# A scan layer's product of state and C, issued on GpSimd as two halves by state with a signal each

## The reference, cut to what matters

```python
dA = jnp.exp(delta[..., None] * A)                        # 512 channels x 16 states
dB = delta[..., None] * Bp[:, :, None, :] * x[..., None]
def step(h, inp):
    dA_t, dB_t, C_t = inp
    h = dA_t * h + dB_t
    return (h, jnp.einsum('bdn,bn->bd', h, C_t))          # y = sum over the 16 states of h * C
...
y = ys + x * D_skip
y = y * jax.nn.silu(z)
return x + jnp.einsum('bli,di->bld', y, out_proj_w)
```

## Time and profile before

| | us |
|---|---|
| median of 3 runs | 461.95 |
| lowest and highest | 460.28 and 463.77 |
| the profiled execution's own time | 461.22 |
| its span, first to last instruction | 459.4 |
| around the span | 1.8 |
| TensorE busy | 399.4 (87%) |
| VectorE busy | 355.5 (77%) |
| GpSimd busy | 291.6 (63%) |
| ScalarE busy | 265.3 (58%) |

### The profile page before, as it was taken

One profiled execution on the slowest core, in us unless ns is written; L12 is line 12 of the kernel. 1 busy time (PEld: TensorE's weight loads), 2 busy tenths in 40 slices (PEclk: granted clock), 3 DMA queues, 4 the chain that ended last, 5 costly groups with the idle time before them and its releaser, 6 DMA issues.

```text
span 459.4 us, 8117 instructions
## 1 busy us (share of the span) xinstructions
PE 399.4 (87%) x2607; PEld 250.9 (55%) x2612; DVE 355.5 (77%) x735; ACT 265.3 (58%) x561; POOL 291.6 (63%) x325
## 2 busy tenths in 40 slices
PE   4999999999999996887699899997779977988874
PEld 2676766767575753443354445464447644556543
DVE  1577877777896789238599997697887799998895
ACT  1466556786957763489652566748441834326563
POOL 0255546364546442229995597989998899994820
PEclk9999999999999999899799999999999999999989
DMA  6960101010100000019400000166000000000001
GB/s 226 389 239 25 47 0 49 1 46 1 49 2 1 1 2 0 1 30 250 114 2 0 0 2 25 55 164 149 0 0 1 2 0 2 0 0 2 11 24 57
DMA packets 22764, 22.64 MB, mean 49 GB/s; under 512 B 1058, under 2 KB 20258, under 8 KB 22212
## 3 DMA queue, kind: packets, MB, share of 16 engines
q1 hardware_dynamic: 22164, 21.65, 15.0%
q10 hardware_dynamic: 560, 0.49, 0.3%
HBM read 21.02 MB, written 1.12 MB: 48 GB/s over the span
## 4 chain that ended last, share of the span: by engine, by line
PE 48%; issue 16%; POOL 15%; DVE 14%; DMA 3%; ACT 1%; SPq 0%; DVEq 0%; POOLq 0%; PEldq 0%; ACTq 0%
POOL both L1649 8%; PE ps L636 7%; PE ps L645 7%; PE ps L444 6%; PE ps L405 5%; PE ps L416 4%; DVE both L1375 3%; PE ps L471 3%; PE ps L505 3%; PE ps L432 3%; POOL both L1602 2%; DMA both<-bounce 2%; DVE zst L1441 2%; PE ps L663 2%; DVE xc L1342 2%
## 5 line engine op out<-in xcount | busy, mean ns | idle before, releaser
L1649 POOL TENSOR_TENSOR both<-both 128x1024 f32<-128x1024 f32 x64 | 149.8, 2361 | 20.1 <-DVE both L1375 19.8
L1375 DVE TENSOR_TENSOR_SCAN both<-both,ps 128x1024 f32<-128x1024 f32 x64 | 144.2, 2277 | 23.4 <-PE ps L636 13.5
L1014 ACT ACTIVATE both<-delta,a_neg 128x504 f32<-128x504 f32 x120 | 74.2, 703 | 39.1 <-DVE both L1375 39.1
L1602 POOL TENSOR_SCALAR both<-both,rden 128x256 f32<-128x256 f32 x128 | 60.1, 484 | 50.7 <-DVE rden L1230 50.7
L645 PEld LDWEIGHTS ps<-con,both 128*128 128x128 f32 x512 | 55.6, 142 | 62.8 <-POOL both L1649 39.8
L645 PE MATMUL ps<-con,both 128*128 128x128 f32 x512 | 70.8, 282 | 13.8 <-POOL both L1649 13.8
L636 PE MATMUL ps<-both 64*128 64x512 f32 x256 | 73.3, 649 | 7.3 <-DVE both L1375 5.8
L887 ACT ACTIVATE both<-both,negmax 128x256 f32<-128x256 f32 x128 | 63.2, 498 | 20.8 <-DVE negmax L1223 20.8
L1223 DVE CUSTOM_DVE_ANT_0 both<-ps,both 128x256 f32<-128x256 f32 x128 | 46.6, 419 | 11.3 <-PE ps L405 11.0
L444 PE MATMUL ps<-both 128*128 128x512 f32 x64 | 33.4, 646 | 6.3 <-DMA both<-in_ctx_t 6.3
L416 PE MATMUL ps<-con,both 128*128 128x128 f32 x256 | 38.5, 277 | 0.0
(11 more groups left out here) (136 smaller groups left out, 611.2 us busy)
## 6 DMA issues: line engine op xcount, KB each, us to landing
both<-bounce SPq DMA_DIRECT2D x16, 512.0 KB, 5.7
both<-in_ctx_t SPq DMA_DIRECT2D x8, 512.0 KB, 3.3
both<-in_wg SPq DMA_DIRECT2D x1, 1024.0 KB, 8.8
both<-in_wu SPq DMA_DIRECT2D x1, 1024.0 KB, 11.0
both<-in_wd SPq DMA_DIRECT2D x1, 1024.0 KB, 12.9
win_sb<-in_win SPq DMA_DIRECT2D x1, 1024.0 KB, 14.8
resid<-in_x SPq DMA_DIRECT2D x1, 896.0 KB, 6.6
both<-in_wkv SPq DMA_DIRECT2D x1, 512.0 KB, 3.8
```

The costliest lines, as they stand in the source:

```text
L1014: act.activation(da[sl % 2].rearrange("p (a s n t) -> p a s n t", a=GT, n=HN, s=2)[:, :, :, n, 1:L], delta[:, idx % RING_X].rearrange("p ( ...
L1375: dve.tensor_tensor_scan(h_sb[:, hu % RING_H], da[e.slot % 2][:, e.tt * HU:(e.tt + 1) * HU], bank(2 * (hu % 2), 2), 0.0, ALU.mult, ALU.add ...
L1602: pool.tensor_scalar(s, s, rden[:, u, q:q + 1], 1.0, ALU.mult, ALU.mult).then_inc(normed, 1)
L1649: pool.tensor_tensor(g_sb[:, hu % RING_G].rearrange("p (n s t) -> p s n t", n=HN, s=2), h_sb[:, hu % RING_H].rearrange("p (s n t) -> p s n ...
```

## The change

`weigh` issues two products instead of one: the first for states 0 to 3 of the round's 8, the second for states 4 to 7. Each is 128 x 512 elements, and each adds one to the semaphore `g_ready`, which now counts two to a round. `accumulate` waits for the first half before its first transpose and for the second half before its fifth. VectorE's scan, which waits for the buffer of three rounds before, and the reload of `cb` for the second group wait for both halves. Nothing else moves.

```diff
@@ SyncE, reload of cb @@
-                            sp.wait_ge(g_ready, count((NC - 1) * NH * GT + b + 1))
+                            sp.wait_ge(g_ready, count(2 * ((NC - 1) * NH * GT + b + 1)))
@@ accumulate @@
-                pe.wait_ge(g_ready, count(hu + 1))
                 for n in range(HN):
+                    if n % (HN // 2) == 0:
+                        pe.wait_ge(g_ready, count(2 * hu + 1 + n // (HN // 2)))
                     mm = pe.matmul(bank(4 + e.idx % 2)[:, e.tt * P:(e.tt + 1) * P], g_sb[:, hu % RING_G, n * P:(n + 1) * P], ident, start=False,
                                    stop=e.nh == NH - 1 and n == HN - 1, is_transpose=True, skip_group_check=True)
                 mm.then_inc(y_acc, 1)
@@ scan @@
-                dve.wait_ge(g_ready, count(hu - RING_H + 1))
+                dve.wait_ge(g_ready, count(2 * (hu - RING_H + 1)))
@@ weigh @@
-                pool.tensor_tensor(g_sb[:, hu % RING_G].rearrange("p (n s t) -> p s n t", n=HN, s=2),
-                                   h_sb[:, hu % RING_H].rearrange("p (s n t) -> p s n t", n=HN, s=2),
-                                   cb[:, e.nh, e.tt].rearrange("p (n s t) -> p s n t", n=HN, s=2), ALU.mult
-                                   ).then_inc(g_ready, 1)
+                for part in range(2):
+                    ns = slice(HN // 2 * part, HN // 2 * (part + 1))
+                    pool.tensor_tensor(g_sb[:, hu % RING_G].rearrange("p (n s t) -> p s n t", n=HN, s=2)[:, :, ns],
+                                       h_sb[:, hu % RING_H].rearrange("p (s n t) -> p s n t", n=HN, s=2)[:, :, ns],
+                                       cb[:, e.nh, e.tt].rearrange("p (n s t) -> p s n t", n=HN, s=2)[:, :, ns],
+                                       ALU.mult).then_inc(g_ready, 1)
```

## The result

| us | before | after |
|---|---|---|
| median of 4 runs each | 461.86 | 466.02 |
| lowest and highest | 460.28 and 463.77 | 464.30 and 466.54 |
| ratio, with its 95% interval | | 1.0092 (1.0059 to 1.0125) |
| the profiled execution, its span | 461.22, 459.4 | 464.30, 462.5 |

One of its twelve executions took 774.59 us, at a granted clock of 1.00; it is left out of the ratio, and nothing here explains it. The forecast was 465.2, so both measurements lie within 0.9 us of it. The profiled executions differ by 3.1 us; the forecast's sum was 3.2.

What follows compares the result with a forecast made beforehand. GpSimd was taken to set the pace in two stretches, TensorE and its waits in another; 0.45 + 1.59 + 0.21 + 0.99 = +3.2 us on the profiled 461.22 gave 464.5, or 465.2 on the median's scale, range 461.5 to 468.5.

Steps and rivals of the forecast that it cites:

- The bound: Scan layer by stretches: TensorE and its waits set the pace 223 to 301 us, GpSimd 301 to 343 and 380 to 406.
- the rounds called covered: Rounds 3 to 26, 41 to 45, 62 and 63: added GpSimd work is absorbed by gaps or other work, 0 us.
- d: Fixed part of a second GpSimd instruction, paid each round: 0.15 us, with 0 to 0.21 kept.
- Rival 1: Second GpSimd instruction nearly free, early signal wins 0.51 us at two handovers: 461.0 us; chance 0.13.
- Rival 2: Fixed part 0.21 us and half the upper bound on TensorE's wait: 6.7 us more, 468.7 us; chance 0.22.
- The second wait: TensorE's wait ahead of its fifth transpose: 0 when already met, upper bound 0.09 us a round, 3.1 us.
- The early signal: Handovers from GpSimd to TensorE at 343.47 and 405.53 us: four transposes left instead of eight, -0.51 us, twice.
- Product 0 to 27: First rounds: three products ahead of `u_of`, which TensorE waits for, +0.45 us; rounds 5 to 26 add 0.
- Rounds 27 to 51: Rounds 27 to 40 +1.59 us after the handover's gain, rounds 46 to 51 +0.21 after a 0.69 gap.
- Rounds 52 to 61: Ten unbroken GpSimd products to the second handover: 1.50 less 0.51, +0.99 us.
- Rival 3: Lateness absorbed between stretches, 343 to 380 us: the 1.59 goes, 1.6 is left, 463.6 us; chance 0.13.
- The overrun gap: Rounds 5 to 26: longest run, five products, adds 0.75 us before a gap of 0.57; taken as 0.

Runs made afterwards that it cites:

- x2: Kernel before, products halved only in rounds 3 to 26, 41 to 45, 62 and 63: 461.91 us against 462.23, ratio 0.9996.
- x3: Kernel before, products halved only in rounds 0 to 2, 27 to 40 and 46 to 61: 465.05 us, ratio 1.0061.
- x9: Kernel before, last `u_of` and one `normal_input` moved later, four B operands (rounds 27 to 30) moved from GpSimd to ScalarE: 458.83 us against 461.86, ratio 0.9929.
- x4: Kernel before with whole products, TensorE waiting again before its fifth transpose for the same count: 461.92 us against 461.89, ratio 1.0008.
- x1: The change, but TensorE waits once, for both halves, before its first transpose: 466.5 us against 462.23 of the kernel before, ratio 1.0076.
- x0: The change once more, with no edit, beside the kernel before: 465.16 us against 462.23, ratio 1.0051.
- x11: Kernel before, products of rounds 40 and 61 alone cut, six states and two: 461.45 us against 461.86, ratio 0.9994.
- x8: Kernel before, last `u_of` moved from round 39 to 45 and one `normal_input` from 53 to 61: 462.11 us against 461.86, ratio 0.9999.

## Why the prediction was right

**The bound** was read rightly. x2 and x3 show it most directly: cuts in the rounds called covered cost nothing, cuts in the others cost all of the 3 us. x9, which takes work off GpSimd in those rounds, is faster.

**d**, put at 0.15 with 0 to 0.21, measured 0.144 by halves and 0.143 by quarters. Rival 1 needed d below 0.04 and falls. The Trainium skill (GPSIMD Engine Reference, 2.1 Instruction dispatch) names tens of cycles for the call of an instruction's routine; the 0.144 us measured here are more than the 0.02 to 0.07 that the prediction estimated from that page, and by the page alone rival 1 would have looked as good as the forecast. Rival 2's 0.21 came from durations, and they mislead here again: 2 x 1.273 - 2.361 = 0.185, with a spacing that says 0.144. So the rule of the Trainium skill to go by start-to-start spacing (Perfetto Trace Analysis, GPSIMD Engine Instruction) agrees with these traces, and was worth 27 x 0.04, 1.1 us, in this case.

**The second wait**, put at 0, is 0 by x4. Rival 2 falls in this part as well.

**The early signal**, put at 0.51 a handover, gave 0.44 (x1 against the change). The term was mis-sized by 0.07, and the reason is in TensorE's timeline. The prediction took half of 1.02 us, the pace of a group of eight with an inflow behind it. At both handovers something else follows, and the prediction's own rows have the eight at 0.93 us there (343.47 to 344.40). Behind the second half the last four take 0.49 (345.89 to 346.38), and 0.93 - 0.49 = 0.44.

**The stages.** Product 0 to 27 was put at +0.45 and measured +0.29, in x0 +0.13 (87.39 against 87.26). `u_of` did move by 3d = 0.43. What is missing lies in the transposes right behind it. TensorE's timeline of the kernel before:

```profile
226.19 1.97 PE L645 MATMUL ps<-con,both 128*128 128x128 f32 x8
228.09 1.17 PE L636 MATMUL ps<-both 64*128 64x512 f32 x4
```

and of the kernel after:

```profile
226.76 1.87 PE L646 MATMUL ps<-con,both 128*128 128x128 f32 x8
228.56 1.13 PE L636 MATMUL ps<-both 64*128 64x512 f32 x4
```

While TensorE stands idle for `u_of`, its granted clock falls to 0.50, the lower of its two levels, and it is back at 1.00 within the microsecond from 228 us on in both kernels, though TensorE went on 0.56 us later in the second. So more of the delayed work runs at the full clock: the eight transposes and the inflow behind them take 1.90 + 1.10 us before, 1.80 + 1.06 after, and 1.62 + 1.06 in x0. That is 0.14 and 0.32 less, and with 0.43 it gives +0.29 and +0.11. The prediction had no term for the clock; it reckoned this stretch at one pace.

The last stage, put at 0, was -0.14 and in x0 +0.03 (52.98 against 52.95), no more than it scatters.

Rounds 27 to 51 were put at +1.80 and measured +1.81, and this nearness is partly luck. In it 20 cuts cost 20d = 2.88, where the prediction had 3.00; 0.44 comes back at the handover, where it had 0.51; and 0.60 of the gap before product 52 was used up (0.69 less the 0.09 that GpSimd needs between the two instructions), where it had all of 0.69. That is 1.84 against 1.80, from three small errors that nearly cancel. Rounds 52 to 61: ten cuts, 1.44 less 0.44 = 1.00, measured 1.01. Rival 3, in which the 343 to 380 us stretch absorbs the lateness, falls: product 52 is late by all of it.

**The overrun gap.** The gap of 0.57 us in the earlier trace rows was overrun, and the run of five became one of seven. The prediction had 0.75 us against this gap and still took 0, while it named the overrun only beside rival 2; five times 0.144 is 0.72. It cost nothing, since the next gap took it up (0.99 us where it was 1.27) and TensorE's transposes stand three rounds behind; x2 shows that.

## What to carry to other kernels

Splitting an instruction to signal earlier paid only where the chain passes to the waiting engine and stays there; in all other rounds it paid nothing, and on the engine that sets the pace each added instruction cost its fixed part. Count those handovers (two of 64 rounds here, 0.44 us each) against the fixed part times the rounds that the splitting engine bounds (27 x 0.144 us), and cut at the handovers alone, or better, take other work off that engine: four spreads moved to ScalarE gave 3 us, while the two small steps moved later, and the cut at the handovers (0.5 a piece in the stages), gave nothing that the times tell. Before moving work, look at what the receiving engine reads at the same time as the others, and at who waits for a step that goes later.

## What the runs showed of the hardware

**The run-to-run scatter goes with TensorE's granted clock.** Runs of the kernel before spread over 5 us, and each run lists its mean granted clock. By it the 29 runs beside x0 group as 464.04 us at 0.982 (4 runs), 462.44 at 0.985 (18), 460.94 at 0.989 (5) and 459.05 at 0.993 (2). The change gives 466.06 at 0.982 (5) and 464.59 at 0.985 (4), +2.0 and +2.2 us at equal clock, and 462.1 at 0.996 (2), for which the kernel before has no run (459.05 at 0.993 is its nearest). Why +2.0 and +2.2 are less than the +2.97 of the stages is open.

In the profiled executions the differences lie in three places. Before the scan layer, product 0 starts between 213.06 and 215.65 us although nothing ahead of it differs: at 213.2 to 213.7 in the kernel before, the change and x2, with a granted clock of 0.96 from 160 to 200 us, at 214.7 to 215.7 in x0, x1, x3, x8 and x9, with 0.91. The second place is the one behind `u_of`, up to 0.3 us. The third is the feed-forward part. From the wait of 1.5 us for `z` (438.31 in the kernel before) to the end it takes 20.49 us in x1, where the clock stays at 1.00; 21.09 in the kernel before and 20.96 in the change, where it falls to 0.50 around 441 and 445 us; 21.73 in x11, around 453; and 22.08 in x8, where it falls right at that wait. TensorE's waits in this part are much the same in all of them, so what decides where the clock falls is open. The row of x1:

```profile
430.00:450.00 20.00, 15.39 (x107) 9.66 (x106) 17.83 (x47) 11.27 (x14) 12.44 (x18) 1.00 0.06 20
```

A stage table that starts behind the first place is steadier than the runs: two traces of the same kernel gave 249.13 both times, with spans of 462.5 and 464.1. Its last stage still holds the third.

**A fixed part of 0.144 us** to an instruction of GpSimd, for float32 products of two SBUF operands, the same at two and at four parts. The two sizes of product give (2.314 - 1.229) / 512 = 2.1 ns an element.

**Where an uneven cut pays.** With transposes of 0.115 us each and a product of 0.29 us a state (2.31 / 8), seven and one (0.27 us won at the handover of round 40) is worse than four and four (0.31) and than six and two (0.51). Five and three was not tried.
